# Expert tokens turned by transposing DMAs on two-byte planes in place of TensorE

## The chip, the cores and the metric

The kernel runs on one core of one Trainium2 chip. The time is the device time in microseconds; the kernel before was run three times. The engines are named as in the profile: PE (TensorE), PEld (its weight loads), DVE (VectorE), ACT (ScalarE), POOL (GpSimd), SP (the engine that issues most DMAs).

## The reference, cut to what matters

The reference is one decoder layer on x of 8 x 512 tokens of 512 floats: an attention form of products only, a cross attention to a context, and a mixture of experts. Each sublayer reads a layer norm of x and adds to x. What the change touches is the last sublayer:

```
x = x + _L0_ffn_ref(_layernorm(x, axis=-1), ...)
# in it: N = 4096 tokens, E = 16 experts, K = 2, F = 704, C = 640 rows an expert
logits = x_tokens @ router_w + router_b;  vals, idx = top_k(softmax(logits), 2)
pos = position of each (token, k) in its expert's queue;  within = pos < C
expert_inputs[e, pos] = x_token                      # gathered rows, zero where unused
expert_outputs = silu(h @ w_gate) * (h @ w_up) @ w_down     # for each expert
out = x + shared_mlp(x) + sum over k of gathered expert_outputs * vals
```

All of it is float32. The kernel makes a float32 product of about full precision from three passes on pairs of parts (a high part rounded to the matmul's format, and a low part, the remainder).

## The kernel before, in words

Phase 1 (function `phase1`) works through the 8 batches of 512 tokens. For every batch it does both attentions, norms the result to y2 (four tiles of 128 tokens x 512), and does three things with y2. `sync` stores y2 to the DRAM table Y (`tokens_normed`, token rows, L272); PE turns y2 into columns and the parts of that are stored to YT (`tokens_normed_T`, L265 and L267); POOL adds y2 to x (L333), and the sum is stored to `out` (L275). From the router's logits slots are worked out and scattered to a slot list by POOL (L348). The steps of neighbouring batches are interleaved by one list, `order`, which every engine walks in the same sequence (written out by hand in `phase2`). "PV" is the step in which y2 and x of a batch are stored and added; on SP it is followed by the load of x three batches on (L235), then by the stores to YT ("Y2T") and the load of the next context ("C", L259). ACT writes the attention's exponentials (step "SC", L445) into the buffer from which YT's high part is stored, so it waits for those stores (`s_ytout`). It makes the next batch's y2 after `s_yout` (the store to Y) and `s_base` (POOL's adds). The last pass of the list has splits of the first weights (`WEIGHTS`) between its steps.

Phase 2 (function `phase2`) has 24 groups: groups 0 to 7 are the shared MLP on a batch of 512 tokens each (four tiles), groups 8 to 23 the experts, 640 rows (five tiles, ET = 5) each. A group has six chunks of F (c = 0 to 5): gate and up products (`three_pass`, L70), then silu on ACT (L1161), product on DVE (L1211), a high part (ACT, L1123) and a low part (DVE, L1196). Then comes the tail of the group: per tile of 128 tokens 17 down products (L1305), a copy-out on DVE (L1236, times the gate value; two banks, so PE's tile n waits for the copy-out of n - 2), and an accumulating scatter by POOL (L1112).

The tail also prepares the next expert's tokens. `tail(g)` yields ("x", g+1, t) before ("down", g, t). In "x", PE transposes the four 128x128 blocks of a gathered tile against the identity into a PSUM bank (`transpose_tile`, L1247), ACT copies the bank to the high part xh (L1123), DVE subtracts for the low part xl (L1187). The next group's first product waits for all of xl. POOL gathers the rows of group g+1 from Y at the start of its work on group g (L1078), into one of two buffers xn, behind the splits of the down weights.

Weights come in chunks of 256 KB, 17 a group of experts (WC), through six raw buffers into a ring of 22 pairs (high part by ACT, L1123, low part by POOL, L1065). SP loads chunk n (L1030) when chunk n - 6 is split (`s_wl`), and a split waits for the last use of the ring place. SP issues them in one plain sequence.

The loop on SP that the change enters is:

```
for n in range(RING, n_chunks):
    load_weights(n)
```

Of the kernel before, what the change touches and what calls it, by code (L numbers as in the profile page):

```python
# [33 lines left out]
U32 = mybir.dt.uint32  # L34
ALU = mybir.AluOpType
# [3 lines left out]
P = 128  # L39
# [34 lines left out]
def build(nc, a):  # L74
    Y = nc.dram_tensor("tokens_normed", (N + PAD, D), F32, kind="Internal").ap()
# [24 lines left out]


def phase1(nc, ctx, a, Y, YT, shared, at):
# [72 lines left out]
    prob = at(88, [NT, S])  # L175
    y2h_rows = [at(88, [NC, S], F32R)] * (B - 2) + [at(38, [NC, S], F32R), at(88, [NC, S], F32R)]
# [47 lines left out]
    s_out, s_yout, s_ytout = sem("s_out"), sem("s_yout"), sem("s_ytout")  # L224
# [5 lines left out]
    def sync(sp):  # L230
# [24 lines left out]
        def step(name, b):  # L255
# [24 lines left out]
    def gpsimd(pool):  # L280
# [26 lines left out]
        for dst in (Y, out):  # L307
            pool.dma_start(dst[N:N + PAD, :].rearrange("(t p) d -> p t d", p=P),
                           vh[:, 0, :].bitcast(F32).unsqueeze(1).to_broadcast([P, PAD // P, D])).then_inc(s_pad, 16)
# [8 lines left out]
        def step(name, b):  # L318
# [7 lines left out]
            if name == "PV":  # L326
# [27 lines left out]
    def scalar(act):  # L354
# [9 lines left out]
        def normalise_x2(b):  # L364
            if b >= 1:
                act.wait_ge(s_yout, 16 * b)
# [495 lines left out]
def phase2(nc, ctx, a, Y, YT, shared, at, attn):  # L862
# [6 lines left out]
    TMP = 3  # L869

# [8 lines left out]
    x_bank = [ps[6], ps[7]]  # L879


# [3 lines left out]
    xn = [at(57, [ET, D]), at(62, [ET, D])]  # L885
    xh, xl = at(52, [NC, CAP], F32R), at(84, [NC, CAP], F32R)
# [9 lines left out]
    s_xg = [sem("t_xg0"), sem("t_xg1")]  # L896
    s_xT, s_xh, s_xl = sem("t_xT"), sem("t_xh"), sem("t_xl")
# [61 lines left out]
    def ring_slot_free(eng, n):  # L959
# [12 lines left out]
        elif n >= 20:  # L972
            eng.wait_ge(attn["s_out"], 16 * (B - 1))
# [39 lines left out]

    def sync(sp):
        step = attn["sync"](sp)

# [28 lines left out]
        sp.wait_ge(attn["s_yout"], 16 * B)  # L1045
# [10 lines left out]
        for n in range(RING, n_chunks):  # L1056
            load_weights(n)
        sp.wait_ge(attn["s_out"], 16 * B)

    def gpsimd(pool):  # L1060
# [10 lines left out]
        def gather(g):  # L1071

            if g <= B + 1:
                pool.wait_ge(s_gu, unit_no[(B - 2, FC - 1, 0)] + 1)
            else:
                pool.wait_ge(s_xT, gathered[g - 1])
            for t in range(ET):
                pool.indirect_dma_start(xn[g % 2][:, t, :], None, Y[:, :], rows_at(groups[g][1], t),  # L1078
                                        bounds_check=N + PAD - 1).then_inc(s_xg[g % 2], 16)
# [7 lines left out]
        for g, (job, part, tiles, last) in enumerate(groups):  # L1087
            if g + 1 < NG and groups[g + 1][0] > 0:
                if g + 1 == B:
                    pool.wait_ge(attn["s_yout"], 16 * B)  # L1090
# [28 lines left out]
    def scalar(act):  # L1119
# [32 lines left out]
        for g in range(NG):  # L1152
# [20 lines left out]
            for what, gx, t in tail(g):  # L1173
                if what == "x":
                    x_hi(gx, t)
# [3 lines left out]
    def vector(dve):  # L1179
        step = attn["vector"](dve)  # L1180

        def x_lo(g, t):
# [3 lines left out]
            src = x_bank[n % 2][:].rearrange("p (c n) -> p c n", c=NC)  # L1186
            dve.tensor_tensor(xl[:, :, cols], src, xh[:, :, cols].bitcast(F32), ALU.subtract).then_inc(s_xl, 1)  # L1187
# [11 lines left out]
        for name, b in order:  # L1199
            if name not in ("RAW", "LOAD", "WEIGHTS"):  # L1200
                step(name, b)
        for g, (job, part, _, _) in enumerate(groups):
# [18 lines left out]
            for what, gx, t in tail(g):  # L1221
                if what == "x":
                    x_lo(gx, t)
# [14 lines left out]
    def tensor(pe):  # L1238
        step = attn["tensor"](pe)

        def transpose_tile(g, t):
            n = gathered[g] + t
            pe.wait_ge(s_xg[g % 2], 16 * ET * ((g - B) // 2 + 1))
            if n >= 2:
                pe.wait_ge(s_xl, n - 1)
            for c in range(NC):
                ins = pe.transpose(x_bank[n % 2][:, c * P:(c + 1) * P], xn[g % 2][:, t, c * P:(c + 1) * P],  # L1247
                                   ident[:])
            ins.then_inc(s_xT, 1)
# [4 lines left out]
        for g, (job, _, tiles, _) in enumerate(groups):  # L1254
# [104 lines left out]
```

## Time and profile before

| | us |
|---|---|
| median of 3 runs | 1942.9 |
| lowest, highest | 1938.39, 1943.36 |
| the profiled execution | 1940.46 |
| its span | 1938.7 |

The profile is of one execution. Its first part gives each engine's busy time in the span, then the span in slices, the DMA queues, the chain of work that ended last, groups of instructions by line, and the DMA issues. A timeline lists instructions in order of time, neighbours of one kind merged; matmuls are pipelined, so in it the distance from start to start is the time that a group takes. "Idle before" is the idle time of an engine ahead of an instruction, and the name behind the arrow is what ended it. A lower-case q behind an engine's name is its instruction queue, where DMAs are issued.

### The profile page before, as it was taken

What the parts mean: (1) busy time and instruction counts of PE and PEld (TensorE: products, weight loads), DVE (VectorE), ACT (ScalarE), POOL (GpSimd) and SP (SyncE); (2) the same over time, 40 slices, a digit from 0 to 9 for tenths busy, and PEclk for the clock granted to TensorE, in tenths of its full rate; (3) what the DMA queues carried; (4) which work ended last, traced back from release to release, by engine and by line L of the source; (5) the groups of instructions that cost most, each with busy time, mean ns of one, the idle gap of its engine ahead of it and who ended that gap; (6) DMA issues with size and microseconds to landing.
All of it is one profiled execution on the core that took longest, in us unless ns stands there. A gap on an engine that the chain in (4) does not pass through costs nothing.

```text
span 1938.7 us, 27725 instructions
## 1 busy us (share of the span) xinstructions
PE 1903.0 (98%) x10672; PEld 1676.6 (86%) x10672; DVE 802.4 (41%) x1896; ACT 668.8 (34%) x1366; POOL 809.2 (42%) x663
## 2 busy tenths in 40 slices
PE   8999999999999999999999999999999999999997
PEld 5788888888877788888899999999999999999996
DVE  2575667567644322222333333333333333333331
ACT  3344544444443111111334333343333433334321
POOL 2133243234353300001556565565655656556531
PEclk9999999999999999999999999999999999999999
DMA  8002321331365333332444554555545555445522
GB/s 273 7 35 97 131 88 66 109 131 41 102 218 179 68 71 68 70 102 43 111 110 124 121 126 97 123 126 120 126 97 121 126 120 128 96 119 130 121 28 27
DMA packets 106738, 203.40 MB, mean 105 GB/s; under 512 B 14800, under 2 KB 14800, under 8 KB 106352
## 3 DMA queue, kind: packets, MB, share of 16 engines
q1 hardware_dynamic: 81312, 148.52, 24.8%
q0 software_dynamic: 25296, 53.11, 16.3%
q8 instruction: 85, 1.39, 0.3%
q14 instruction: 45, 0.37, 0.1%
HBM read 135.92 MB, written 65.68 MB: 104 GB/s over the span
## 4 chain that ended last, share of the span: by engine, by line
PE 68%; DVE 1%; ACT 1%; issue 0%; POOL 0%; ACTq 0%; DVEq 0%; POOLq 0%
PE ps L70 44%; PE ps L1305 22%; PE ps L1247 2%; ACT buffer L1123 0%; DVE buffer L1196 0%; ACT buffer L361 0%; DVE buffer L1211 0%; DVE stats L492 0%; ACT lg L422 0%; PE ps L702 0%; ACT buffer L1161 0%; PE ps L708 0%; POOL out_tokens L1112 0%; ACT L1161 0%; DVE buffer L638 0%
## 5 line engine op out<-in xcount | busy, mean ns | idle before, releaser
L70 PE MATMUL ps<-buffer,buffer 128*128 128x320 f32 (+1 forms) x6816 | 1221.7, 340 | 7.4 <-DVE buffer L603 2.1
L70 PEld LDWEIGHTS ps<-buffer,buffer 128*128 128x128 f32 x6816 | 1104.6, 188 | 110.1 <-DVE buffer L603 2.3
L1065 POOL TENSOR_TENSOR buffer<-buffer,buffer 128x512 fp32r<-128x512 f32 x289 | 387.4, 1504 | 219.9 <-ACT buffer L1123 219.6
L1305 PE MATMUL ps<-buffer,buffer 128*128 128x512 f32 x1904 | 458.5, 395 | 3.5 <-DVE buffer L1196 3.5
L1305 PEld LDWEIGHTS ps<-buffer,buffer 128*128 128x128 f32 x1904 | 352.3, 189 | 76.6 <-POOL buffer L1065 3.2
L1211 DVE TENSOR_TENSOR buffer<-ps,buffer 128x320 f32<-128x320 f32 (+1 forms) x240 | 127.5, 532 | 597.9 <-ACT buffer L1161 555.1
L1161 ACT ACTIVATE buffer<-ps 128x320 f32<-128x320 f32 (+1 forms) x240 | 112.3, 468 | 656.0 <-PE ps L70 635.1
L1123 ACT ACTIVATE buffer<-buffer 128x512 fp32r<-128x512 f32 (+3 forms) x529 | 269.6, 563 | 56.8 <-PE ps L1305 50.5
L1112 POOL DMA_INDIRECT out_tokens<-buffer,slot_index x80 | 125.5, 1569 | 219.8 <-DVE buffer L1236 207.3
L1196 DVE TENSOR_TENSOR buffer<-buffer,buffer 128x320 fp32r<-128x320 f32 (+1 forms) x240 | 183.3, 764 | 12.0 <-ACT buffer L1123 10.8
L356 ACT ACTIVATE buffer<-ps 128x512 fp32r<-128x512 f32 (+1 forms) x212 | 112.7, 605 | 108.9 <-PE ps L70 42.9
L324 POOL TENSOR_TENSOR buffer<-buffer,buffer 128x512 fp32r<-128x512 f32 x32 | 41.0, 1314 | 243.1 <-ACT buffer L356 243.1
L1105 POOL DMA_DIRECT2D out_tokens<-buffer x32 | 27.5, 860 | 256.0 <-DVE buffer L1233 252.1
L1236 DVE TENSOR_SCALAR buffer<-ps,slot_list 128x512 f32<-128x512 f32 x80 | 60.1, 751 | 174.0 <-PE ps L1305 173.9
L1123 ACT ACTIVATE buffer<-ps 128x512 fp32r<-128x512 f32 x80 | 47.6, 594 | 203.3 <-PE ps L1247 203.3
L361 ACT ACTIVATE buffer<-buffer,shift,rstd 128x512 f32<-128x512 f32 x96 | 70.4, 805 | 124.0 <-DVE shift L505 124.0
L1078 POOL DMA_INDIRECT buffer<-tokens_normed,slot_index x80 | 84.2, 1052 | 22.3 <-issue 22.3
L348 POOL DMA_INDIRECT slots<-pairs,slot_u x64 | 65.3, 1020 | 32.8 <-issue 17.7
L333 POOL TENSOR_TENSOR buffer<-buffer,buffer 128x512 f32<-128x512 f32 x32 | 40.4, 1292 | 66.6 <-DVE shift L505 53.5
L492 DVE BATCH_NORM_STATS2 stats<-buffer 128x6 f32<-128x512 f32 x96 | 61.2, 682 | 13.1 <-DMA buffer<-in_x 12.6
L1187 DVE TENSOR_TENSOR buffer<-ps,buffer 128x512 fp32r<-128x512 f32 x80 | 55.3, 691 | 23.2 <-ACT buffer L1123 23.2
L708 PE MATMUL ps<-ident,buffer 128*128 128x128 f32 x512 | 61.2, 273 | 0.2 <-ACT buffer L445 0.2
(110 smaller groups left out, 945.4 us busy)
## 6 DMA issues: line engine op xcount, KB each, us to landing
buffer<-in_wts SPq DMA_DIRECT2D x289, 256.0 KB
tokens_normed_T<-buffer SPq DMA_DIRECT2D x16, 1024.0 KB
buffer<-tokens_normed_T SPq DMA_DIRECT2D x16, 1024.0 KB, 7.4
buffer<-in_x SPq DMA_DIRECT2D x8, 1024.0 KB, 6.6
buffer<-in_ctxT SPq DMA_DIRECT2D x8, 1024.0 KB, 12.6
tokens_normed<-buffer SPq DMA_DIRECT2D x8, 1024.0 KB, 4.6
out_tokens<-buffer SPq DMA_DIRECT2D x8, 1024.0 KB, 4.5
out_tokens<-buffer POOLq DMA_DIRECT2D x32, 256.0 KB
```

The lines of the kernel that those rows point to most:

```text
L70: last = pe.matmul(out, left, right, start=(i == 0), stop=(i == len(todo) - 1))
L348: pool.indirect_dma_start(slots[:, :], bass.IndirectOffsetOnAxis(ap=slot_u[:, b, k, t:t + 1], axis=0), pairs[:, b, k, t, :], None, bounds_ ...
L356: return act.activation(dst, src, ACT.Copy)
L361: act.activation(dst[:, t, :], x[b % XS][:, t, :], ACT.Identity, bias=shift[k][:, t:t + 1], scale=rstd[k][:, t:t + 1]).then_inc(done, 1)
L1065: pool.tensor_tensor(wl[n % RING][:], wraw[n % RAW][:], wh[n % RING][:].bitcast(F32), ALU.subtract).then_inc(s_wl, 1)
L1078: pool.indirect_dma_start(xn[g % 2][:, t, :], None, Y[:, :], rows_at(groups[g][1], t), bounds_check=N + PAD - 1).then_inc(s_xg[g % 2], 16)
L1112: pool.indirect_dma_start(out[:, :], rows_at(part, t), ost[:, t, :], None, bounds_check=N + PAD - 1, compute_op=ALU.add).then_inc(s_add[t] ...
L1123: return act.activation(dst, src, ACT.Copy)
L1161: act.activation(silu[u % TMP][0:rows_of(c), 0:n], bank[0:rows_of(c), 0:n], ACT.Silu)\
L1196: dve.tensor_tensor(lo[:, first:first + n], ht[u % TMP][0:rows, 0:n], hh[0:rows, c, first:first + n].bitcast(F32), ALU.subtract).then_inc( ...
L1211: dve.tensor_tensor(ht[u % TMP][0:rows_of(c), 0:n], up_bank[u % 2][rows, 0:n], silu[u % TMP][0:rows_of(c), 0:n], ALU.mult).then_inc(s_ht, 1)
L1305: ins = pe.matmul(down_bank[n % 2][:], left, right, start=(c == 0 and i == 0), stop=(c == FC - 1 and i == len(passes) - 1))
```

## The change

The token table Y holds, instead of 512 floats per token, the upper 16 bits of all 512 and then the lower 16 bits of all 512 (1024 two-byte numbers, the same bytes). In phase 1 POOL writes these two planes for each tile of y2, two copies a tile behind the four adds of step "PV", into one of two buffers (four in the last batch), and SP stores Y in four DMAs of 256 KB each behind them. In phase 2 the gathers fetch the same rows into one buffer. SP issues five transposing DMAs per expert (one a tile, 128 rows of 1024 two-byte numbers into eight blocks of 128x128), between the loads of weight chunks RING + 17 job + 9 and + 10. PE's transposes are gone. In the tail ACT writes the upper halves (x_top) and DVE the lower halves (x_low) of every float of the turned tile into xw, which shares its place with xl; then ACT makes xh from it and DVE xl in place.

Phase 1:

```diff
             if name == "PV":
                 rows = slice(b * S, (b + 1) * S)
-                sp.wait_ge(s_y2, NT * (b + 1))
-                sp.wait_ge(s_yout, 16 * b)
-                sp.dma_start(Y[rows, :].rearrange("(t p) d -> p t d", p=P), y2[:]).then_inc(s_yout, 16)
                 sp.wait_ge(s_base, NT * (b + 1))
                 sp.wait_ge(s_out, 16 * b)
                 sp.dma_start(out[rows, :].rearrange("(t p) d -> p t d", p=P), x[b % XS][:]).then_inc(s_out, 16)
+                for t in range(NT):
+                    sp.wait_ge(s_halves, NT * b + t + 1)
+                    sp.dma_start(Y[b * S + t * P:b * S + (t + 1) * P, :],
+                                 halves(b, t)[:].rearrange("p two d -> p (two d)")).then_inc(s_yout[t % 2], 16)
...
+                if b == B - 1:
+                    pool.wait_ge(s_out, 16 * (B - 1))
+                for t in range(NT):
+                    n = NT * b + t
+                    if n >= 2:
+                        pool.wait_ge(s_yout[t % 2], 16 * (n // 2))
+                    words = y2[:, t, :].bitcast(U16).rearrange("p (d two) -> p d two", two=2)
+                    for half in range(2):
+                        last = pool.tensor_copy(halves(b, t)[:, half, :], words[:, :, 1 - half])
+                    last.then_inc(s_halves, 1)
...
         def normalise_x2(b):
             if b >= 1:
-                act.wait_ge(s_yout, 16 * b)
+                act.wait_ge(s_halves, NT * b)
```

Phase 2:

```diff
+    TURN_AT = RAW + 4
-    xn = [at(57, [ET, D]), at(62, [ET, D])]
-    xh, xl = at(52, [NC, CAP], F32R), at(84, [NC, CAP], F32R)
+    xn = at(57, [ET, 2 * D], U16)
+    xp = [at(62 + t, [2 * NC, P], U16) for t in range(ET)]
+    xh, xl, xw = at(52, [NC, CAP], F32R), at(84, [NC, CAP], F32R), at(84, [NC, CAP])
...
+    def halves_of(t):
+        return xw[:, :, t * P:(t + 1) * P].bitcast(U16).rearrange("p c (n two) -> p c n two", two=2)
+    def expert_tokens_free(eng, g):
+        eng.wait_ge(s_gu, unit_no[(g - 1, FC - 1, len(cuts(g - 1)) - 1)] + 1)
...
+        def turn_tokens(g):
+            sp.wait_ge(s_xg, 16 * gathered[g + 1])
+            if gathered[g]:
+                sp.wait_ge(s_xtop, gathered[g])
+                sp.wait_ge(s_xlow, gathered[g])
+            for t in range(ET):
+                sp.dma_start_transpose(xp[t][:], xn[:, t, :]).then_inc(s_xp, 16)
...
         for n in range(RING, n_chunks):
+            job, i = divmod(n - RING, WC)
+            if i == TURN_AT and job < E:
+                turn_tokens(B + job)
             load_weights(n)
...
-                pool.wait_ge(s_xT, gathered[g - 1])
+                pool.wait_ge(s_xp, 16 * gathered[g])
...
+        def x_top(g, t):
+            copy(halves_of(t)[:, :, :, 1], xp[t][:, 0:NC, :]).then_inc(s_xtop, 1)
         def x_hi(g, t):
-            act.wait_ge(s_xT, n + 1)
-            copy(xh[:, :, cols], x_bank[n % 2][:].rearrange("p (c n) -> p c n", c=NC)).then_inc(s_xh, 1)
+            act.wait_ge(s_xtop, n + 1)
+            act.wait_ge(s_xlow, n + 1)
+            copy(xh[:, :, cols], xw[:, :, cols]).then_inc(s_xh, 1)
...
             for what, gx, t in tail(g):
                 if what == "x":
+                    if t == 0:
+                        act.wait_ge(s_xp, 16 * gathered[gx + 1])
+                        expert_tokens_free(act, gx)
+                        x_top(gx, t)
+                    if t + 1 < ET:
+                        x_top(gx, t + 1)
                     x_hi(gx, t)
...
+        def x_low(g, t):
+            dve.tensor_copy(halves_of(t)[:, :, :, 0], xp[t][:, NC:2 * NC, :]).then_inc(s_xlow, 1)
         def x_lo(g, t):
-            dve.tensor_tensor(xl[:, :, cols], src, xh[:, :, cols].bitcast(F32), ALU.subtract).then_inc(s_xl, 1)
+            dve.tensor_tensor(xl[:, :, cols], xw[:, :, cols], xh[:, :, cols].bitcast(F32), ALU.subtract)\
+                .then_inc(s_xl, 1)
...
-        def transpose_tile(g, t):
-            n = gathered[g] + t
-            pe.wait_ge(s_xg[g % 2], 16 * ET * ((g - B) // 2 + 1))
-            if n >= 2:
-                pe.wait_ge(s_xl, n - 1)
-            for c in range(NC):
-                ins = pe.transpose(x_bank[n % 2][:, c * P:(c + 1) * P], xn[g % 2][:, t, c * P:(c + 1) * P],
-                                   ident[:])
-            ins.then_inc(s_xT, 1)
...
             for what, gx, t in tail(g):
                 if what == "x":
-                    transpose_tile(gx, t)
                     continue
```

DVE walks its tail in the same way as ACT, with x_low in the place of x_top and x_lo in that of x_hi. Where waits on `s_yout` stood, in phase 2 they are now on both of its semaphores.

## Rows read from the trace of the kernel before

**Rows 1.** The page, part 1: busy us (share of span) x instructions.

```profile
PE 1903.0 (98%) x10672; PEld 1676.6 (86%) x10672; DVE 802.4 (41%) x1896; ACT 668.8 (34%) x1366; POOL 809.2 (42%) x663
```

**Rows 2.** The page, part 4: chain that ended last, shares by line.

```profile
PE ps L70 44%; PE ps L1305 22%; PE ps L1247 2%; ACT buffer L1123 0%; DVE buffer L1196 0%; ACT buffer L361 0%; DVE buffer L1211 0%; DVE stats L492 0%; ACT lg L422 0%; PE ps L702 0%; ACT buffer L1161 0%; PE ps L708 0%; POOL out_tokens L1112 0%; ACT L1161 0%; DVE buffer L638 0%
```

**Rows 3.** Timeline of PE, one expert: start us, length us, instructions.

```profile
1444.61 38.88 PE L70 MATMUL ps<-buffer,buffer 128*128 128x320 f32 x264
1483.32 0.60 PE L1247 MATMUL ps<-ident,buffer 128*128 128x128 f32 x4
...
1487.65 0.60 PE L1247 MATMUL ps<-ident,buffer 128*128 128x128 f32 x4
...
1505.00 1.18 PE L70 MATMUL ps<-buffer,buffer 128*128 128x320 f32 x7
```

**Rows 4.** Timeline of the last expert: DVE's first and fifth copy-out.

```profile
1910.20 0.75 DVE L1236 TENSOR_SCALAR buffer<-ps,slot_list 128x512 f32<-128x512 f32 x1 [1.77 <-PE ps L1305]
...
1925.62 0.75 DVE L1236 TENSOR_SCALAR buffer<-ps,slot_list 128x512 f32<-128x512 f32 x1 [3.10 <-PE ps L1305]
```

**Rows 5.** Timeline of POOL, the expert of rows 3.

```profile
1455.62 1.16 POOL L1078 DMA_INDIRECT buffer<-tokens_normed,slot_index  x1 [0.16 <-issue]
...
1461.10 1.02 POOL L1078 DMA_INDIRECT buffer<-tokens_normed,slot_index  x1 [0.31 <-issue]
1462.15 2.55 POOL L1065 TENSOR_TENSOR buffer<-buffer,buffer 128x512 fp32r<-128x512 f32 x2
```

**Rows 6.** Busy time by stretch; last columns: granted clock, DMA share, GB/s.

```profile
1465.00:1467.00 2.00, 2.00 (x16) 2.00 (x15) 0.54 (x3) 1.02 (x3) 0.00 (x0) 1.00 0.76 223
1467.00:1469.00 2.00, 2.00 (x16) 2.00 (x15) 0.41 (x2) 0.82 (x2) 1.62 (x2) 1.00 0.03 11
```

**Rows 7.** Groups by line: busy us, mean ns, idle before.

```profile
L1123 ACT ACTIVATE buffer<-ps 128x512 fp32r<-128x512 f32 x80 | 47.6, 594 | 203.3 <-PE ps L1247 203.3
...
L1187 DVE TENSOR_TENSOR buffer<-ps,buffer 128x512 fp32r<-128x512 f32 x80 | 55.3, 691 | 23.2 <-ACT buffer L1123 23.2
...
L339 POOL TENSOR_TENSOR buffer<-buffer,buffer 128x512 f32<-128x512 f32 x32 | 40.3, 1291 | 45.9 <-ACT buffer L361 45.9
...
L305 POOL MEMSET buffer<- 128x512 f32 x1 | 0.5, 514 | 0.0
```

**Rows 8.** The page, part 6: DMA issue, KB, us to landing.

```profile
buffer<-in_bv SPq DMA_DIRECT2D x1, 256.0 KB, 2.9
```

**Rows 9.** DMA of 456:471 us, with slot scatters; and a stretch of full load.

```profile
DMA packets 633, 0.87 MB, mean 58 GB/s; under 512 B 224, under 2 KB 224, under 8 KB 630
...
q0 software_dynamic: 224, 0.01, 1.2%
...
429.00:431.00 2.00, 2.00 (x11) 1.65 (x10) 1.79 (x15) 0.00 (x0) 0.00 (x0) 1.00 1.05 408
```

**Rows 10.** Timeline of a middle batch: SP's stores, ACT's exponentials, PE behind them.

```profile
413.81 0.38 SPq L275 DMA_DIRECT2D out_tokens<-buffer  x1
...
418.96 0.50 SPq L265 DMA_DIRECT2D tokens_normed_T<-buffer  x1
...
432.29 0.69 ACT L445 ACTIVATE buffer<-ps,nbias 128x512 f32<-128x512 f32 x1 [4.37 <-DVE nbias L621]
...
438.16 0.69 ACT L445 ACTIVATE buffer<-ps,nbias 128x512 f32<-128x512 f32 x1 [1.94 <-DVE nbias L621]
...
440.82 1.91 PE L708 MATMUL ps<-ident,buffer 128*128 128x128 f32 x16
```

**Rows 11.** Timeline around the last batch's exponentials: POOL, SP, ACT, PE.

```profile
540.53 5.04 POOL L333 TENSOR_TENSOR buffer<-buffer,buffer 128x512 f32<-128x512 f32 x4 [4.16 <-DVE buffer L594]
...
548.53 0.48 SPq L265 DMA_DIRECT2D tokens_normed_T<-buffer  x1
...
558.98 0.69 ACT L445 ACTIVATE buffer<-ps,nbias 128x512 f32<-128x512 f32 x1 [4.92 <-DMA tokens_normed_T<-buffer]
...
564.99 1.97 PE L708 MATMUL ps<-ident,buffer 128*128 128x128 f32 x16 [0.18 <-ACT buffer L445]
```

More of the change, by code:

```diff
@@ L34 @@
 U32 = mybir.dt.uint32
+U16 = mybir.dt.uint16
 ALU = mybir.AluOpType
@@ L74, in build @@
 def build(nc, a):
-    Y = nc.dram_tensor("tokens_normed", (N + PAD, D), F32, kind="Internal").ap()
+    Y = nc.dram_tensor("tokens_normed", (N + PAD, 2 * D), U16, kind="Internal").ap()
     YT = nc.dram_tensor("tokens_normed_T", (2, B, D, S), F32, kind="Internal").ap()
@@ L175, in phase1, with halves @@
     prob = at(88, [NT, S])
+    halves_rows = [at(96, [2, D], U16), at(97, [2, D], U16)]
+    halves_last = [at(46 + t, [2, D], U16) for t in range(NT)]
+    def halves(b, t):
+        return halves_last[t] if b == B - 1 else halves_rows[t % 2]
     y2h_rows = [at(88, [NC, S], F32R)] * (B - 2) + [at(38, [NC, S], F32R), at(88, [NC, S], F32R)]
@@ L223, in phase1 @@
     s_fill = sem("s_fill")
-    s_out, s_yout, s_ytout = sem("s_out"), sem("s_yout"), sem("s_ytout")
+    s_out, s_yout, s_ytout = sem("s_out"), [sem("s_yout0"), sem("s_yout1")], sem("s_ytout")
+    s_halves = sem("s_halves")
     s_zero, s_pad = sem("s_zero"), sem("s_pad")
@@ L306, in gpsimd @@
         pool.wait_ge(s_zero, 1)
-        for dst in (Y, out):
+        for dst, dt in ((Y, U16), (out, F32)):
+            zeros = vh[:, 0, :].bitcast(dt)
             pool.dma_start(dst[N:N + PAD, :].rearrange("(t p) d -> p t d", p=P),
-                           vh[:, 0, :].bitcast(F32).unsqueeze(1).to_broadcast([P, PAD // P, D])).then_inc(s_pad, 16)
+                           zeros.unsqueeze(1).to_broadcast([P, PAD // P, zeros.shape[1]])).then_inc(s_pad, 16)
         pool.wait_ge(s_pad, 32)
@@ L878, in phase2 @@
     down_bank = [ps[4], ps[5]]
-    x_bank = [ps[6], ps[7]]
     wraw = [at(i, [D]) for i in range(RAW)]
@@ L895, in phase2 @@
     s_xn = [sem("t_xn0"), sem("t_xn1")]
-    s_xg = [sem("t_xg0"), sem("t_xg1")]
-    s_xT, s_xh, s_xl = sem("t_xT"), sem("t_xh"), sem("t_xl")
+    s_xg, s_xp, s_xtop, s_xlow = sem("t_xg"), sem("t_xp"), sem("t_xtop"), sem("t_xlow")
+    s_xh, s_xl = sem("t_xh"), sem("t_xl")
     s_gu, s_silu, s_ht, s_hh, s_hl = sem("t_gu"), sem("t_silu"), sem("t_ht"), sem("t_hh"), sem("t_hl")
@@ L972, in ring_slot_free @@
         elif n >= 20:
-            eng.wait_ge(attn["s_out"], 16 * (B - 1))
+            for stored in attn["s_yout"]:
+                eng.wait_ge(stored, 16 * NT * B // 2)
     def split_after(g, step):
@@ L1044, in sync @@
         sp.wait_ge(attn["s_base"], NT * B)
-        sp.wait_ge(attn["s_yout"], 16 * B)
         step("Y2T", B - 1)
@@ L1071, in gather @@
         def gather(g):
-            if g <= B + 1:
+            if g == B:
                 pool.wait_ge(s_gu, unit_no[(B - 2, FC - 1, 0)] + 1)
             else:
-                pool.wait_ge(s_xT, gathered[g - 1])
+                pool.wait_ge(s_xp, 16 * gathered[g])
             for t in range(ET):
-                pool.indirect_dma_start(xn[g % 2][:, t, :], None, Y[:, :], rows_at(groups[g][1], t),
-                                        bounds_check=N + PAD - 1).then_inc(s_xg[g % 2], 16)
+                pool.indirect_dma_start(xn[:, t, :], None, Y[:, :], rows_at(groups[g][1], t),
+                                        bounds_check=N + PAD - 1).then_inc(s_xg, 16)
         for name, b in order:
@@ L1089, in gpsimd @@
                 if g + 1 == B:
-                    pool.wait_ge(attn["s_yout"], 16 * B)
+                    for stored in attn["s_yout"]:
+                        pool.wait_ge(stored, 16 * NT * B // 2)
                     pool.wait_ge(s_index, 1)
@@ L1185, in x_lo @@
             cols = slice(t * P, (t + 1) * P)
-            src = x_bank[n % 2][:].rearrange("p (c n) -> p c n", c=NC)
-            dve.tensor_tensor(xl[:, :, cols], src, xh[:, :, cols].bitcast(F32), ALU.subtract).then_inc(s_xl, 1)
+            dve.tensor_tensor(xl[:, :, cols], xw[:, :, cols], xh[:, :, cols].bitcast(F32), ALU.subtract)\
+                .then_inc(s_xl, 1)
         def h_lo(u):
@@ L1201, in vector @@
                 step(name, b)
+        for stored in attn["s_yout"]:
+            dve.wait_ge(stored, 16 * NT * (B - 1) // 2)
         for g, (job, part, _, _) in enumerate(groups):
@@ L1222, in vector @@
                 if what == "x":
+                    if t == 0:
+                        dve.wait_ge(s_xp, 16 * gathered[gx + 1])
+                        expert_tokens_free(dve, gx)
+                        x_low(gx, t)
+                    if t + 1 < ET:
+                        x_low(gx, t + 1)
                     x_lo(gx, t)
```

## The prediction

> **What bounds the kernel now.** I read the totals first: PE is busy for 98% of the span [rows 1], so only what shortens PE's own stream, or makes it wait, can move the time. The chain of waits says the same and names PE's lines: 44% the three-pass products, 22% the down projection, 2% L1247, the transposes that this change takes away [rows 2]. The timeline of PE shows one expert (job) of the sixteen: 38.71 us of gate and up products from 1444.61, then five down tiles from 1483.32 to 1505.00, each headed by four transposes, 60.4 us from one job to the next [rows 3]. Nothing else ends last here. So I ask what a tile costs without transposes, whether the DMA that replaces them is in time for the same tail, and what the added work of the first half does to PE there.
>
> **1. Transposes off PE.** With them a down tile takes (1505.00 - 1483.32) / 5 = 4.336 us [rows 3]. The last job has no successor to prepare, so its tiles come bare: their results are copied out at 1910.20 to 1925.62, (15.42) / 4 = 3.855 us apart [rows 4]. That is 0.481 us for four transposes, much less than their busy time, since they overlap. 16 jobs x 5 tiles x 0.481 = 38.5 us. They stand on the path that sets the end, and a job becomes 38.71 + 5 x 3.855 = 58.0 us.
>
> **2. What takes their place in the tail.** Per tile ACT gets one more copy (x_top) and DVE one more (x_low), both two-byte data, 128x512. The trace shows none of that kind. Nearest are ACT's 594 ns and DVE's 691 ns copies of 128x512 [rows 7]. A denser or a wider access could make it half or double. I take 0.6 and 0.7. DVE then has 0.7 + 0.69 + 0.75 = 2.1 us per tile, ACT 1.2, against PE's 3.855; at double, 2.8. Hidden behind the down products either way. x_lo of the fifth tile follows the copy-out of the fourth, while PE works on the fifth: as now. Cost nothing.
>
> **3. The DMA path's due time.** The gathers of the next job's tokens are issued by POOL at 1455.62 to 1462.1, behind six weight splits [rows 5]; DMA traffic falls from 223 to 11 GB/s at 1467.0 [rows 6], so they have landed 22.4 us into the job. SP has by then come to the turn (it stands behind the load whose slot is freed by the split at 1462.15 to 1464.7 [rows 5]), so the five transposing DMAs go out at 22.4 us. Queued behind them on SP is chunk 32 of the ring and everything after; ACT splits that chunk before it touches the tokens. When are they late? DVE's x_low stands in front of the copy-out of down tile 0, and down tile 2 needs the bank of tile 0. Tile 2 would start at 1483.32 + 2 x 3.855 = 1491.0. Before it: chunk 32 lands and is split (1.3), two x_top (1.2), x_hi (0.6), x_lo (0.69), copy-out (0.75), together 4.5. So the turned tokens must lie by 1486.5: 19.5 us for five DMAs, 3.9 us each. If they take d each and are late, a job lasts 22.4 + 5d + 4.5 + three tiles (11.6) = 38.5 + 5d, which equals today's 60.4 at d = 4.4. Beyond this point each us of d costs 80 us in all. The weight ring itself is 22 chunks for 17 of a job, so the held loads alone don't starve PE.
>
> **d has no row.** From below: 256 KB at the 408 GB/s that the queue reaches is 0.64 us [rows 9]. The scatters of 8-byte pairs cost 1.2% of 16 engines x 15 us / 224 packets = 13 ns a packet [rows 9]. If a turn moves pieces of 256 bytes (128 two-byte elements, 1024 pieces, 64 an engine), a piece is 13 ns + 256 bytes at 25.5 GB/s per engine (10 ns) = 23 ns, d = 1.5 us, with a latency like the 2.9 us of the small load once [rows 8]: 5 x 1.5 + 2.9 = 10.4 of 19.5 us. If pieces are 32 bytes (squares of 16 elements), 512 an engine at 13 ns: d = 6.7. If it is done element by element, 8192 an engine: 107 us, the far end. I take d about 2, nearest the rows of the widest pieces that the layout allows (a row of a block is contiguous in the source), and keep the rest as a rival. Cost nothing.
>
> The Trainium skill ("DMA: Bandwidth & Descriptors", its bandwidth tables) has a transposing DMA at 261 GB/s on one kernel, an estimate of d = 1.0 us here, which leaves the sum as it is. Against this change speaks "VectorE: DVE Perf Modes" (The three transpose paths): 1309 ns for 128x128 two-byte elements by DMA, an estimate of 8 x 1.309 = 10.5 us for a tile of eight blocks if they follow one another; by it the job would be 91 us and the kernel near 2435 us. No row of before decides between the two pages.
>
> **4. First half: the planes.** POOL gets eight copies of 128x512 per batch behind its four adds, and SP stores Y in four pieces behind them. A copy lies between the memset's 0.51 and the 1.29 us of the two-input add [rows 7]; I take 0.9. In a middle batch SP stores the sum at 413.81, which is when the adds are done. Then two pairs of copies to 417.4, their stores land 2.9 us later [rows 8], two more pairs to 422.6, then x's load and the store of YT at 423.5 instead of 418.96: 4.5 us later (3.5 to 6 for the ends). Behind YT waits ACT's exponential (its buffer). The queue carried x and YT, 3 MB at 408 GB/s, till about 428.5 [rows 9, 10]; the exponentials start at 432.29, the fourth at 438.16, and PE needs them at 440.82 [rows 10]. Allowed is a shift of some 8 us, needed 4.5. Cost nothing in seven batches. The gains of ACT (it waits for the copies instead of a store) free nothing on PE.
>
> **The last batch has no such slack.** POOL's adds end at 545.57, SP stores YT at 548.53, ACT's exponential already waits for it and starts at 558.98, and PE's transposes of the probabilities wait for ACT and start at 564.99 [rows 11]. With 8 x 0.9 us of copies and one wait for a store, POOL is free at 554.1; the first two splits and the loads that wait for them follow, YT goes out at 557.2 with 2 MB behind a shorter queue and lands near 564.5. Four exponentials at 0.87 end at 568.1 instead of 564.8: PE waits 3.3 us more. Ends: 0 and 6. The copies of batch 7 lie before splits and scatters that nobody needs for 20 us; nothing.
>
> **Sum.** 1938.7 - 38.5 + 3.3 = 1903.5 us of span; the profiled run took 1.8 us more than its span, so 1905.3. That run is 2.4 us under the median of the three shown, so I say 1906 us; against the median that is 1.9% faster.
>
> **The rivals.**
> A. Turning is slow (slower than before). One mechanism: five transposing DMAs overrun the 19.5 us in front of the tail, DVE stands at x_low, the bank of tile 0 isn't emptied, PE stops before down tile 2, sixteen times. It decides from d = 4.4. With 32-byte pieces, d = 6.7: 72.0 us a job, 1938.7 + 3.3 + 16 x 11.6 + 1.8 = 2129 us. For it: no row holds d under 4.4, and the gathers land only 22.4 us into the job [rows 6]. Against: what SP would load meanwhile waits behind the transposes, so they have the DMA engines nearly for themselves. The 1309 ns of the Trainium skill's "VectorE: DVE Perf Modes" (The three transpose paths), as estimated in step 3, is this rival at its 2435 us.
> B. Partly late, d of 3.9 to 4.6: the 2.4 us a job are given back. 1915 to 1950; in the middle, no change, 1943.
> C. The planes cost PE in every batch: POOL's two-byte stepped copies take over 1.5 us each, YT comes more than 8 us late and the exponentials with it. At 2.5 us a copy the shift is some 15 us, 7 us x 7 batches on top: 1955. Against it: POOL's two-input add of this size takes 1.29 us [rows 7].
> D. The change doesn't do what it says: the down tile stays at 4.3 us for another reason (weight loads, banks). The last job's tiles exclude it [rows 4].
>
> **Chances.** My forecast 0.58 (its own range 1897 to 1915). B 0.10, of which 0.04 end faster and 0.06 within 0.3%. A 0.27, mostly between 1960 and 2450. C 0.05. D under 0.01. Faster by over 0.3% (6 us, about what a measurement of this kernel can tell from none) 0.62, same 0.06, slower 0.32. The range runs from 1895 to 2130: it takes in B, C and A up to 32-byte pieces, and leaves out slower turning, some 0.15.
>
> **What would show it.** Right: PE busy falls, L1247 is gone, the down tiles start 3.86 us apart and jobs 58.0 us; in the tail ACT and DVE wait for PE as now; the transposing DMAs land before 1480 on this clock. Step 4: one pause of 3 us more on PE before the transposes at 565 and none in other batches. Wrong: DVE's or ACT's first plane copy waits for a DMA, with PE idle in front of down tile 2 in each of 16 jobs (A, B); exponentials that wait for the YT store in every batch (C). The clock is granted in full (1.00, 2.4 GHz) in the rows that show it [rows 6, 9]; I count on no change.

## The result, and the profile after

| | before | changed |
|---|---|---|
| median of 4 runs, us | 1943.13 | 1908.62 |
| lowest, highest | 1938.39, 1943.46 | 1906.54, 1909.04 |
| profiled execution: time, span | 1940.46, 1938.7 | 1906.54, 1904.8 |

The changed kernel takes 0.9826 of the time (95% interval 0.9809 to 0.9843), 1.8% less. 1906 was forecast, with faster as the likeliest.

The page of the changed kernel, parts 1 and 4 (they answer to [rows 1, 2]; the three-pass products are now L71, the down products L1353):

```profile
PE 1866.0 (98%) x10352; PEld 1642.1 (86%) x10352; DVE 861.2 (45%) x1976; ACT 726.2 (38%) x1446; POOL 847.8 (45%) x727
...
PE ps L71 45%; PE ps L1353 22%; ACT buffer L1161 0%; DVE buffer L1247 0%; ACT buffer L381 0%; DVE buffer L1264 0%; DVE stats L512 0%; ACT lg L442 0%; PE ps L722 0%; ACT buffer L1203 0%; PE ps L728 0%; POOL out_tokens L1150 0%; ACT L1203 0%; DVE oh L682 0%; DVE buffer L658 0%
```

The 320 transposes are gone, nothing has taken their place in the chain, and PE is still busy for 98%. The timeline of PE over one job of the changed kernel (for [rows 3]):

```profile
1427.35 38.88 PE L71 MATMUL ps<-buffer,buffer 128*128 128x320 f32 x264
1466.06 19.57 PE L1353 MATMUL ps<-buffer,buffer 128*128 128x512 f32 x85
```

The next job starts at 1485.48: 58.1 us a job instead of 60.4, with one unbroken run of 85 down products. The DMA path of the same job, as SP's timeline shows it, and the answer for the transposing line in that window:

```profile
1453.14 6.80 SPq L1050 DMA_TRANSPOSE buffer<-buffer  x5
```

```profile
L1050 SPq DMA_TRANSPOSE buffer<-buffer x5: 1242/1339/1384, 1453.1 to 1458.6; - x5
...
DMA to landing us min/median/max: 3.2/3.4/3.6
```

The five are issued 25.8 us into the job, 1.34 us apart, and each lands 3.4 us after its issue: all lie at 1462.0, 4 us before PE even begins the down products. What they are made of stands in part 3 of the page and its packet line:

```profile
DMA packets 191603, 224.36 MB, mean 118 GB/s; under 512 B 99664, under 2 KB 99664, under 8 KB 191216
...
q1 hardware_dynamic: 166176, 169.51, 30.8%
```

Before, 14800 packets were under 512 B and q1 had 24.8%. So a DMA has (99664 - 14800) / 80 = 1061 small packets, the 1024 pieces of 256 bytes (and a few more), and they cost (30.8% of 1904.8 - 24.8% of 1938.7) x 16 / 84864 = 20 ns each.

From PE's starts the 33.9 us of the span can be told apart. The gather-side tails: 15 jobs went from 60.41 to 58.16 us and the first tail gave 1.9, together -35.6. At the start of phase 2's last shared group (911.53 before, 914.00 after) the changed kernel is 2.5 us behind. That is the sum of a start that was 2.1 us quicker, two longer pauses of PE in the last pass of phase 1 (+2.0 and +1.4), and stretches at the lower clock that lie elsewhere (+2.6 at 596, -1.6 at 671, where only the kernel before has one). The last 0.8 us come from the last job's end.

The two pauses, in the changed kernel's waits of PE (before they were 2.3 and 0.2):

```profile
PE ps L722 <- DVE picked L685: 3.8, 1, 3.8
PE ps L728 <- ACT buffer L465: 2.2, 1, 2.2
```

The second is the one of [rows 11]. The first has POOL beside it. DVE's one-hots of the router, before and then in the changed kernel, and what POOL does meanwhile in the latter (timelines):

```profile
592.53 0.36 DVE L662 TENSOR_TENSOR oh<-iota_e,eidx 128x64 f32<-128x64 f32 x2
```

```profile
592.84 1.13 DVE L682 TENSOR_TENSOR oh<-iota_e,eidx 128x64 f32<-128x64 f32 x2
...
592.17 2.27 POOL L353 COPY buffer<-buffer 128x512 uint16<-128x512 uint16 x4
```

The same two instructions take three times as long beside POOL's plane copies. Then the clock. Busy time by stretch of the changed kernel, the granted clock third from the end:

```profile
592.00:596.00 4.00, 0.59 (x15) 0.50 (x15) 3.79 (x14) 0.91 (x3) 2.44 (x5) 0.84 0.72 269
596.00:600.00 4.00, 4.00 (x10) 3.13 (x11) 3.73 (x10) 1.07 (x2) 2.82 (x5) 0.50 0.51 189
600.00:604.00 4.00, 4.00 (x16) 3.22 (x15) 1.29 (x5) 0.00 (x0) 2.69 (x3) 0.80 0.19 68
```

After a stretch in which PE was nearly idle its clock is granted at half (1.2 instead of 2.4 GHz), and 24 products take 8.4 us instead of 5.7. How much of that is the change's doing these two traces can't tell; the run without planes, below, shows that most of it is not.

In a middle batch (for [rows 10]; POOL's adds end at 411.7) the timelines of POOL and SP read:

```profile
411.62 2.27 POOL L353 COPY buffer<-buffer 128x512 uint16<-128x512 uint16 x4
418.49 2.28 POOL L353 COPY buffer<-buffer 128x512 uint16<-128x512 uint16 x4 [4.60 <-DMA tokens_normed<-buffer]
```

```profile
411.70 0.38 SPq L280 DMA_DIRECT2D out_tokens<-buffer  x1
412.81 8.31 SPq L283 DMA_DIRECT2D tokens_normed<-buffer  x4
...
421.64 0.57 SPq L273 DMA_DIRECT2D tokens_normed_T<-buffer  x1
```

The store of YT comes 9.9 us behind that of the sum, 5.2 before. ACT's exponentials now wait for it in six batches, and nobody on PE waits for ACT:

```profile
ACT buffer L465 <- DMA tokens_normed_T<-buffer: 37.2, 6, 7.3
```

### The profile page after: what moved, and what is told of

Read it like the earlier page. It is cut to its first block, busy times and chain, and to the rows that moved or that the text cites. A ratio compares the mean times of both kernels' runs of the same rounds, so it can differ in the third digit from the quotient of the medians.

```text
span 1904.8 us, 27457 instructions
## 1 busy us (share of the span) xinstructions
PE 1866.0 (98%) x10352; PEld 1642.1 (86%) x10352; DVE 861.2 (45%) x1976; ACT 726.2 (38%) x1446; POOL 847.8 (45%) x727
## 2 busy tenths in 40 slices
DMA packets 191603, 224.36 MB, mean 118 GB/s; under 512 B 99664, under 2 KB 99664, under 8 KB 191216
## 3 DMA queue, kind: packets, MB, share of 16 engines
q1 hardware_dynamic: 166176, 169.51, 30.8%
q8 instruction: 82, 1.34, 0.3%
## 4 chain that ended last, share of the span: by engine, by line
PE 67%; DVE 1%; ACT 1%; issue 0%; POOL 0%; ACTq 0%; DVEq 0%; POOLq 0%
PE ps L71 45%; PE ps L1353 22%; ACT buffer L1161 0%; DVE buffer L1247 0%; ACT buffer L381 0%; DVE buffer L1264 0%; DVE stats L512 0%; ACT lg L442 0%; PE ps L722 0%; ACT buffer L1203 0%; PE ps L728 0%; POOL out_tokens L1150 0%; ACT L1203 0%; DVE oh L682 0%; DVE buffer L658 0%
## 5 line engine op out<-in xcount | busy, mean ns | idle before, releaser
L71 PE MATMUL ps<-buffer,buffer 128*128 128x320 f32 (+1 forms) x6816 | 1224.2, 341 | 7.4 <-DVE buffer L623 2.1
L71 PEld LDWEIGHTS ps<-buffer,buffer 128*128 128x128 f32 x6816 | 1106.5, 188 | 110.8 <-DVE buffer L623 2.3
L1353 PE MATMUL ps<-buffer,buffer 128*128 128x512 f32 x1904 | 439.1, 390 | 4.1 <-DVE buffer L1247 4.0
L1161 ACT ACTIVATE buffer<-buffer 128x512 fp32r<-128x512 f32 (+4 forms) x689 | 374.1, 595 | 172.5 <-PE ps L1353 90.9
L1353 PEld LDWEIGHTS ps<-buffer,buffer 128*128 128x128 f32 x1904 | 355.1, 188 | 82.3 <-issue 5.8
L1231 DVE COPY buffer<-buffer 128x512 uint16<-128x512 uint16 x80 | 71.4, 913 | 0.5
L728 PEld LDWEIGHTS ps<-ident,buffer 128*128 128x128 f32 x512 | 57.3, 140 | 4.8 <-ACT buffer L465 2.7
```

What stands on the lines that cost most here:

```text
L71: last = pe.matmul(out, left, right, start=(i == 0), stop=(i == len(todo) - 1))
L728: last = pe.transpose(bank_of(step, b, c)[:, t * P:(t + 1) * P], src[:, t, c * P:(c + 1) * P], ident[:])
L1161: return act.activation(dst, src, ACT.Copy)
L1231: dve.tensor_copy(halves_of(t)[:, :, :, 0], xp[t][:, NC:2 * NC, :]).then_inc(s_xlow, 1)
L1353: ins = pe.matmul(down_bank[n % 2][:], left, right, start=(c == 0 and i == 0), stop=(c == FC - 1 and i == len(passes) - 1))
```

## The experiments

The experiments ran in three sets, each on one chip and with the kernel before beside it, whose median was 1941.4 us in the first set, 1941.5 in the second and 1940.8 in the third. The changed kernel itself ran ahead of them (1908.62, with the kernel before at 1943.13) and once more in the third set (1910.50). The sets were on different chips, so a difference between two of them is less sure than one within a set. Differences below are of medians; the ratios in brackets are against the kernel before of the same set, with their 95% intervals.

**PE's transposes alone.**

```diff
 # before.py, tensor(): the tail
                 if what == "x":
-                    transpose_tile(gx, t)
+                    if gathered[gx] + t < 2:
+                        transpose_tile(gx, t)
                     continue
 # ACT's x_hi waits for the gather and for s_xl instead of s_xT; the gather for s_xh
```

> The kernel before with PE's transposes of the gathered tokens left out (all but the first two tiles; ACT and DVE copy whatever stands in the banks, so the experts work on the wrong tokens); nothing else of the change. Theory (step 1 of the prediction, transposes cost what the last job's bare tiles lack): 58.0 us a job, 38 us less than before, some 1905 us. Rival (the changed kernel's jobs, 58.16 us in its trace, are all that a tail can do): 58.16 us a job, 35.6 us less, 1907 us.

Measured: 1905.79 us (0.9825, 0.981 to 0.984), 35.6 us less; PE's three-pass products of neighbouring jobs start at 1423.47 and 1481.63, and PE's timeline of this kernel has:

```profile
1462.19 19.60 PE L1310 MATMUL ps<-buffer,buffer 128*128 128x512 f32 x85
1481.63 24.65 PE L70 MATMUL ps<-buffer,buffer 128*128 128x320 f32 x167
```

The rival was right: 58.15 us a job without any plane or transposing DMA. So the tail of the changed kernel is as short as a tail from which the transposes are just left out, and my 58.0 was the pace of the last job, which isn't that of the others: its 85 down products take 19.45 us in both traces, those of the other jobs 19.57 to 19.61 (one 19.84). The trace of the changed kernel shows a likely reason, which no run tests by itself: DVE's last low part before the tail takes 0.82 us beside POOL's weight splits, and PE's weight loads stand for 0.26 us until it is done (timeline, changed kernel). In the last job, which has no splits, the same operation takes 0.49, and PE's weight loads don't stand.

```profile
1468.55 0.82 DVE L1247 TENSOR_TENSOR buffer<-buffer,buffer 64x320 fp32r<-64x320 f32 x1 [0.68 <-ACT buffer L1161]
1469.40 2.88 DVE L1231 COPY buffer<-buffer 128x512 uint16<-128x512 uint16 x2
1469.49 15.72 PEld L1353 LDWEIGHTS ps<-buffer,buffer 128*128 128x128 f32 x70 [0.26 <-issue]
```

**The planes alone, on the kernel before.**

```diff
 # phase1 of the changed kernel with phase2 of the kernel before, and in it
-xn = [at(57, [ET, D]), at(62, [ET, D])]
+xn = [at(57, [ET, 2 * D], U16), at(62, [ET, 2 * D], U16)]     # transposed as F32 views
 # POOL: both copies take words[:, :, 1]
```

> The kernel before with the planes of the first half alone: POOL's eight copies a batch (both of them copy the upper halves, so the table holds no true tokens) and Y's stores in four parts behind them; gathers of the same bytes, PE's transposes as before. Theory (they cost PE only in the last pass: 2.0 us behind the YT store, 1.4 us from POOL's copies beside DVE's router steps, and what the clock loses after the longer pause, up to 2.6): 2 to 6 us slower than before, 1945 to 1949 us; the batches before the last keep their pace of 67.7 us. Rival (a cost in every batch): 14 us or more slower. Rival (no cost; the differences in the trace are chance): within 1 us.

Measured: 1942.69 us, 1.0014 (1.0005 to 1.0023): slower, by 1.3 us of the medians and 2.7 by the ratio. PE's wait at the picks is that of the changed kernel (3.8 us); before the transposes of the probabilities it is only 0.9 us, so this run has one of the two longer pauses and little of the other. The clock is at 0.52 behind the picks. No cost per batch (67.67 us from one to the next, as before): the rival C of the prediction is out.

**The transposing DMAs without the planes.**

```diff
 # the changed kernel
-for t in range(NT): ... pool.tensor_copy(halves(b, t)[:, half, :], words[:, :, 1 - half])
-for t in range(NT): ... sp.dma_start(Y[...], halves(b, t)...)
+sp.wait_ge(s_y2, NT * (b + 1))                  # at the old place of the store
+for k in range(2):
+    sp.dma_start(Y[two tiles], konst broadcast).then_inc(s_yout[k], 16)
```

> The changed kernel without POOL's plane copies: Y is stored from a constant, in two DMAs a batch of the same bytes, at the place that the store had before (so the gathered tokens are a constant); phase 2 with its transposing DMAs as in the change. Theory: 3 to 6 us faster than the changed kernel, 1903 to 1905 us. Rival (the planes cost nothing): 1908 to 1909 us.

Measured: 1905.86 us (0.9826, 0.9812 to 0.9839), 35.5 us less than before. That is 2.8 us less than the changed kernel's first median of 1908.62, just short of the 3 to 6 that I expected, and 4.6 less than its second, 1910.50; against the kernel before beside each, the first ratio of the changed kernel is the same 0.9826 and the second 0.9845. By whole runs the planes cost something between nothing and 5 us. The trace says more. PE's waits are back to those of the kernel before (0.2 us before the transposes of the probabilities), and behind the picks PE's timeline has:

```profile
PE ps L720 <- DVE picked L683: 2.4, 1, 2.4
```

```profile
593.13 7.38 PE L71 MATMUL ps<-buffer,buffer 128*128 128x512 f32 x24 [0.85 <-DVE buffer L1262]
```

Without any plane the 24 products take 7.38 us, and 7.34 in the run with PE's transposes alone taken out, whose first half is that of the kernel before. The 5.74 us at full clock in the trace of the kernel before are the exception among all these traces: 1.6 of the 2.6 us by which the changed kernel is slower there are lost without any plane as well.

**The turn 14 us later, and 7 us later.**

```diff
-            if i == TURN_AT and job < E:
+            if i == (TURN_AT + 4 if job < E - 1 else TURN_AT) and job < E:
```

> The changed kernel with the five transposing DMAs issued four chunks later (behind the split that ends chunk step c = 3, 14 us later; the last job keeps its place). It measures what the cover is. By step 3 of the prediction with the trace's own length of the five (landed 11 us after the first is issued, some 35.5 us into the job): they land at 49.6 us, and 4.5 + 11.6 us follow, 65.7 us a job instead of 58.16, 15 times: +113 us, about 2020 us. Rival (what the trace shows as DMA time is other traffic, and five take 5 us): 59.7 us a job, +23 us, 1931 us. Rival (the down products don't wait for the turned tokens as I say): no change.

Measured: 2032.94 us, 124 us over the changed kernel. A job of the trace starts at 1503.88; timelines of PE, SP and DVE:

```profile
1542.59 8.05 PE L1353 MATMUL ps<-buffer,buffer 128*128 128x512 f32 x34
1556.93 14.38 PE L1353 MATMUL ps<-buffer,buffer 128*128 128x512 f32 x51 [6.29 <-DVE buffer L1295]
1571.15 9.10 PE L71 MATMUL ps<-buffer,buffer 128*128 128x320 f32 x61
```

```profile
1544.15 7.53 SPq L1050 DMA_TRANSPOSE buffer<-buffer  x5
```

```profile
1553.50 0.79 DVE L1231 COPY buffer<-buffer 128x512 uint16<-128x512 uint16 x2 [7.60 <-DMA buffer<-buffer]
```

The mechanism of rival A to the letter: DVE stands at x_low, the bank of tile 0 isn't emptied, PE pauses before down tile 2. The tokens lie at 49.6 us, as computed. The two terms behind it differ: 3.4 us instead of 4.5 from there to tile 2, and 14.2 instead of 11.6 for three tiles, since PE's clock falls to 0.50 after the pause (4 us later by the rows of busy time). The 14 jobs with this tail last 66.5 us in the mean against 65.7.

> The changed kernel with the five transposing DMAs two chunks later (7 us), the last job as it is. By the measured 25.8 us into the job for the issue and 9.2 us for the five they then land at 42.0 us, and with 4.5 + 11.6 us behind them the job is 58.1 us: just at the edge, 0 to 15 us slower than the changed kernel. Rival (the cover is narrower than the law says): 30 us or more slower.

Measured with TURN_AT + 2: 1910.66 us against 1910.50 of the changed kernel beside it. The job of 1432.20, timelines of SP and PE:

```profile
1465.03 6.80 SPq L1050 DMA_TRANSPOSE buffer<-buffer  x5
```

```profile
1470.92 19.60 PE L1353 MATMUL ps<-buffer,buffer 128*128 128x512 f32 x85
1490.36 9.84 PE L71 MATMUL ps<-buffer,buffer 128*128 128x320 f32 x66
```

The five land just as x_low begins (1474.25), and the job is 58.16 us. So the cover is at least 7 us longer than used, and gone before 14.

**What turning costs the DMA engines.**

```diff
-sp.dma_start_transpose(xp[t][:], xn[:, t, :]).then_inc(s_xp, 16)
+sp.dma_start(xp[t][:].rearrange("p c n -> p (c n)"), xn[:, t, :]).then_inc(s_xp, 16)
```

> The changed kernel with the five transposing DMAs of a job replaced by plain DMAs of the same tiles (same source, place and bytes; the blocks stay unturned, so the experts work on the wrong numbers). Theory (the turn is hidden: the five land some 10 us after their issue, with more than half of the cover left): same time as the changed kernel within 2 us, 1907 to 1909 us, while the DMA engines' busy share in a job falls. Rival (the transposing DMAs hold back weight loads or gathers somewhere, unseen in the waits): 4 us or more faster.

Measured: 1910.39 us; 1908.62 and, in the third set, 1910.50 for the changed kernel: no gain. Busy time over one job, changed kernel and then plain copies (DMA share next to last):

```profile
1427.35:1485.50 58.15, 58.15 (x351) 54.61 (x350) 25.59 (x39) 24.95 (x51) 35.59 (x27) 1.00 0.63 145
```

```profile
1431.00:1489.15 58.15, 58.15 (x351) 54.61 (x350) 25.65 (x39) 24.96 (x51) 35.64 (x27) 1.00 0.59 145
```

The turn adds 0.04 x 58.15 = 2.3 us of all engines per job, over a plain copy of the same bytes. SP issues a plain copy in 0.60 us (median of a job's five) and a turning one in 1.34; both land 3.4 us after their issue.

**Where the planes' cost lies: three moves.**

```diff
 # YT first: SP's step "PV" for b < B - 1
                 sp.dma_start(out[rows, :]..., x[b % XS][:]).then_inc(s_out, 16)
+                if b < B - 1:
+                    store_YT(b)              # then the four Y stores; step "Y2T" skips it
```

> The changed kernel with SP's two YT stores of batches 0 to 6 moved in front of the Y stores (and of x's load) of their batch. Theory (2.0 us of PE's pause at 565 in the trace come from the YT store that stands behind the plane stores): that pause is gone, 1 to 2 us faster than the changed kernel, some 1907 us; the waits of ACT for YT go back to almost none. Rival (what PE lacks there is another thing, the first weight loads or their splits): no difference.

Measured: 1910.80 us, no faster (the changed kernel in the third set: 1910.50). ACT's waits for YT are gone as expected, but PE's pause grew from 2.2 to 3.8 us. ACT's timeline of this kernel:

```profile
563.61 0.64 ACT L1166 ACTIVATE buffer<-buffer 128x512 fp32r<-128x512 f32 x1 [10.77 <-DMA buffer<-in_wts]
```

My theory fell, the rival stands: ahead of the exponentials ACT splits weight chunks 6 and 7. Their loads wait for POOL's splits 0 and 1, which stand behind the plane copies, which wait for the Y stores. Whatever delays the Y stores delays that.

```diff
 # POOL, step "PV" of the last batch, ahead of the plane copies
+                    pool.wait_ge(s_pick, B - 1)
```

> The changed kernel with POOL's plane copies of the last batch held until DVE has written the router's picks of batch 6 (one wait on POOL). Theory (POOL's two-byte copies beside DVE's small router steps stretch them by 1.4 us, PE pauses 3.8 instead of 2.3 us, and after the longer pause its clock is granted at half for some 7 us): the pause is 2.3 us again, the clock stays, 1.5 to 4 us faster than the changed kernel, 1905 to 1907 us. Rival (DVE is slowed by something else there): the pause stays at 3.8 us, no difference.

Measured: 1908.12 us (1907.78 to 1911.68). PE's waits of this kernel have:

```profile
PE ps L723 <- DVE picked L686: 2.3, 1, 2.3
```

The pause is back at 2.3 us, and DVE's two one-hots take 0.36 us again, so POOL's copies are what stretched DVE's router steps. The clock isn't restored: 0.69 in 598 to 602, and 24 products take 7.35 us (8.38 in the changed kernel, 5.74 before), as in the runs without planes. The gain in time is under what these runs can tell.

Both moves together:

> The changed kernel with both moves: YT's stores ahead of the Y stores, and the last batch's plane copies behind the router's picks. Theory: all that the planes cost comes back, 3 to 5 us faster than the changed kernel, 1904 to 1906 us, as fast as the run without plane copies (1905.9). Rival (the last batch's copies, now later, delay splits and scatters that somebody waits for): no faster than the better of the two moves.

Measured: 1909.47 us, no better than the better one: pauses of 3.7 and 2.4 us, each where its move puts it.

```diff
 # POOL's copies and SP's Y stores of batch 6 move from step "PV" to a step of their own
-"Q": [("WEIGHTS", (2, 6)), ("WEIGHTS", (6, 8))]
+"Q": [("WEIGHTS", (2, 6)), ("WEIGHTS", (6, 8)), ("PLANES", B - 2)]
+                    pool.wait_ge(s_pick, B - 1)      # last batch, as above
```

> The changed kernel with two moves: POOL's plane copies of batch 6 and SP's Y stores of it stand behind the first eight weight splits (instead of ahead of them), and the last batch's wait for the router's picks, as in the run before. Theory, mended by the YT-first run (PE's pause before the transposes of the probabilities comes from weight splits 0 and 1, loads 6 and 7 and YT, all behind the plane copies): that pause is 0.2 to 1 us as in the kernel before, the pause at the picks 2.3 us, 2 to 4 us faster than the changed kernel run beside it, 1904 to 1907 us. Rival (the copies, now beside DVE's maxima, stretch those, and the pause stays): no difference.

> The changed kernel once more, on the same chip as the two others of this call: 1907 to 1911 us, with PE's pauses of 2.2 us before the transposes of the probabilities and 3.8 us at the picks.

Measured beside each other, five runs each: 1905.73 us (1902.47 to 1907.48) with the moves and 1910.50 (1908.98 to 1913.67) without; against the kernel before 0.9822 (0.9808 to 0.9835) and 0.9845 (0.9831 to 0.9858). PE's waits in the kernel with the moves:

```profile
PE ps L727 <- DVE picked L690: 2.4, 1, 2.4
...
PE ps L733 <- ACT buffer L470: 0.6, 1, 0.6
```

Both pauses are back to nearly what they were before (3.8 and 2.5 us without the moves). The five times with the moves all lie below the five without, 4.8 us by the medians, and the version is far below the kernel before; it isn't told from the first times of the changed kernel (1906.54 to 1909.04).

The pauses themselves are 3.3 us. The clock adds to that, and here the first trace of the changed kernel was lucky. The 96 products behind the pause before the transposes of the probabilities, without the moves and then with them (timelines of PE):

```profile
573.92 23.68 PE L71 MATMUL ps<-buffer,buffer 128*128 128x512 f32 x96 [1.53 <-DVE buffer L648]
```

```profile
570.30 22.07 PE L71 MATMUL ps<-buffer,buffer 128*128 128x512 f32 x96 [1.54 <-DVE buffer L653]
```

In the six traces in which that pause is 0.2 to 1.1 us (the kernel before, the runs with the transposes out, with the planes only, without planes, with the turn 14 us later, and this version) they take 22.0 to 22.1 us. Of the seven with 2.2 to 3.8 us five have 23.6 to 24.1, and the YT-first run lost 1.3 us in the transposes ahead of them; only the first trace of the changed kernel lost nothing.

The two profiles also differ by their first 47 us, in which the granted clock is 0.67 and 0.60 of full from 37 on and 0.83 in the first profile of the changed kernel. By a group of 48 three-pass products that every kernel has near 550 us, and that starts at 549.68 in the first profile of the changed kernel, 551.78 in the kernel before, and 552.81 and 554.54 with and without the moves, single executions are up to 4.9 us apart before either pause, and all of that arises in the first 90 us.

## Why the prediction was right

By its steps:

**Step 1, transposes off PE.** Right, the size a little high: 38.5 us were taken, 35.6 came by PE's starts, and with nothing but the transposes removed also 35.6 by the medians. A job gave 2.25 us instead of 2.41, and the first tail 1.9. The term was mis-sized because the bare tiles were read from the last job [rows 4], whose down products go a little faster (19.45 us against 19.57 or more); that the others have weight splits beside them is the likely reason.

**Step 2, the tail's extra copies cost nothing.** Right. x_low took 0.45 us alone and up to 1.5 beside POOL, more than the doubled value that I allowed, and 58.16 us a job with them equal 58.15 without.

**Step 3, the due time and d.** Right. Issue at 25.8 us instead of 22.4: SP came to it only behind the next pair of POOL's splits, those of 1450.12 to 1452.67 in the job above, one pair later than I read from [rows 5]. The pieces of 256 bytes were the right guess: 1061 packets, 20 ns each (23 taken); 1.34 us a DMA instead of 2, and 3.4 to landing (2.9 taken). 1061 packets of 20 ns on 16 engines are 1.3 us, and SP takes 1.34 us to issue one; which of the two sets the pace these runs don't tell. The first run that was meant to break the cover did it with the job length that the law gives, within 1 us, though two of its terms were off in opposite directions, and the second came near its edge. Of the Trainium skill's two figures the 261 GB/s of "DMA: Bandwidth & Descriptors" (Latency and other measured facts) is the nearer: 256 KB in 1.34 us are 196 GB/s at issue pace. The Trainium skill's 1309 ns for 128x128 ("VectorE: DVE Perf Modes", The three transpose paths) can't be multiplied by the blocks of one DMA: eight blocks took 3.4 us from issue to landing, not 10.5.

**Step 4, the planes.** The cost per batch was nothing, as said; YT is 4.8 us later (4.5 computed), and that nearness is luck: the copies took 0.57 us (0.9 taken), and the first of the stores freed POOL only 5.7 us after its issue (2.9 taken; 3.9 in the last pass, and what makes the difference is not shown). The pause in the last pass was +2.0 instead of +3.3, and its cause was named only in part: the YT-first run shows that the chain of splits and loads is enough by itself. What the step didn't see is the other end, where I wrote "nothing": POOL's copies of batch 7 slow DVE's router steps, 1.4 us. Nor did it see the clock, of which I expected no change: behind the longer pause before the transposes of the probabilities 1.3 to 2.5 us are lost in most of the traces. The planes' price is then 3.4 us of pauses and in most executions 1.6 more, near the 4.8 us by which the version with the moves is faster, against 3.3 in the sum. The planes on the kernel before cost less, since there the one pause hardly grew.

The sum was 1903.5 us of span against 1904.8, and that nearness is part luck: 2.9 us too much gain in step 1 and some 1.2 too little cost of pauses and clock were met by a start that was 2.1 us quicker in this one execution and 0.8 us at its end. The medians, 1908.6 and 1910.5 against the 1906 forecast, show the errors more plainly. Rival A's price held where it was provoked (66.5 us a job for a computed 65.7), with the two terms behind the tokens 1.1 us shorter and 2.6 us longer than computed. It didn't happen because d (1.34 us from issue to issue) is a third of the 4.4 us where it begins. Two sums of the rivals are off and change nothing: by its own terms A at 10.5 us a tile is 2433 us, not 2435, and B's d of 3.9 to 4.6 spans 1905 to 1961, not 1915 to 1950.

## What to carry to other kernels

A transpose that PE does between products costs PE only its distance from start to start (35.6 / 320 = 0.11 us for a 128x128 float32 block here, less than half of its listed 272 ns), and moving it to DMA was worth just that here, where the DMAs had a due time with room. Work out such a due time from the first in-order engine that stands at the new data and what waits behind it, then move the issue on purpose to find the edge. A copy put onto an engine that has time to spare is not free when another engine's small steps or in-order weight splits stand beside or behind it: put it behind them. And before a difference between two traces is put down to the change, look at the same place in every other trace: the stretch at half clock behind the picks was in kernels without the change too, and the loss behind the other pause was missing from the first trace alone.

## What the runs showed of the hardware that I had not expected

Beside POOL's two-byte copies of 128x512 DVE's operations of 128x64 took three times as long (0.36 to 1.13 us for two), and DVE's own two-byte copy took 0.45 us alone and up to 1.5 us beside POOL's float32 subtractions. After pauses of PE its clock was granted at 0.50 for some microseconds, but not after each of equal length: behind the pause of 2.3 to 2.4 us at the picks the 24 products took 7.3 to 7.4 us in five traces and 5.74 in that of the kernel before, which kept 1.00, and behind one of 3.8 us 7.1 to 8.7. What decides it these runs leave open.

SP took 1.34 us to issue a turning DMA of 256 KB and 0.60 us for a plain one of the same bytes, while both landed 3.4 us after their issue.
